# A gated cross-attention and expert layer on one core: new orders within a slot, the first two tiles' queries by one projection and transfers, and fewer identity matmuls

## The reference

```python
# x [32,128,128], ctx [32,77,96], 16 heads of 8
x = x + tanh(g_xattn) * xattn(layernorm(x), ctx)      # layer norms, q, k, v, softmax over 77 keys
x = x + tanh(g_ffn) * ffn(layernorm(x))
# ffn: logits = x @ w_router; top 2 of 8 experts, gates = softmax of the two
#      y_e = square(relu(x @ w1[e])) @ w2[e];  out = sum of gate_e * y_e
```

## Time and profile before

| | us |
|---|---|
| median of 3 runs | 349.1 (348.03 to 349.65) |
| the profiled execution, whole | 348.87 |
| its span | 347.1 |
| TensorE busy | 292.9 (84%) |
| VectorE busy | 230.6 (66%) |
| ScalarE busy | 181.0 (52%) |
| GpSimd busy | 109.2 (31%) |
| mean granted TensorE clock (1 is full) | 0.966 |

### The profile page before, as it was taken

The page is one execution under the profiler, slowest core; times in us unless marked ns, Lnnn a source line. Parts: engine busy times, 40 slices in busy tenths (PEclk is TensorE's granted clock), DMA queues, the critical chain, the costliest instruction groups (busy, mean ns, idle before and its releaser), DMA issues.

```text
span 347.1 us, 7792 instructions
## 1 busy us (share of the span) xinstructions
PE 292.9 (84%) x2809; PEld 237.6 (68%) x2809; DVE 230.6 (66%) x929; ACT 181.0 (52%) x412; POOL 109.2 (31%) x198
## 2 busy tenths in 40 slices
PE   0867979888889998999899989999999999787695
PEld 0435658666767877777777777777777788675484
DVE  7565275677757775778677757886657656554555
ACT  1331354656455566555655566466556555553373
POOL 6495305147303531343134313421322100211000
PEclk9995587999999999999999999999999999999999
DMA  3243011027343836283629281835273530350011
GB/s 82 79 128 111 19 42 34 17 54 129 118 178 57 126 111 213 53 132 105 216 49 124 54 281 35 117 66 157 115 113 54 153 126 3 81 198 0 0 34 30
DMA packets 18918, 32.92 MB, mean 95 GB/s; under 512 B 4921, under 2 KB 12058, under 8 KB 18880
## 3 DMA queue, kind: packets, MB, share of 16 engines
q1 hardware_dynamic: 12176, 23.39, 28.0%
q0 software_dynamic: 3216, 7.66, 9.2%
q10 hardware_dynamic: 3488, 1.38, 1.5%
HBM read 21.04 MB, written 2.21 MB: 67 GB/s over the span
## 4 chain that ended last, share of the span: by engine, by line
PE 46%; DVE 27%; issue 9%; DMA 6%; ACT 6%; POOL 3%; SPq 2%; DVEq 0%; ACTq 0%; POOLq 0%
PE y L592 10%; PE c L547 8%; DVE u L1122 6%; PE ab L503 4%; DMA gb<-gates_scratch 3%; PE ab L570 2%; DMA qs<-q_lo 2%; PE ab L445 2%; DVE negm L1003 2%; POOL rs L1288 2%; PE s L524 2%; PE ab L453 2%; PE ab L562 2%; PE h L478 2%; PE h L458 2%
## 5 line engine op out<-in xcount | busy, mean ns | idle before, releaser
L1003 DVE TENSOR_REDUCE negm<-ab 128x4 f32<-128x308 f32 x128 | 60.6, 474 | 53.3 <-PE ab L503 52.8
L804 ACT ACTIVATE p<-s 77x512 f32<-77x512 f32 x128 | 74.2, 583 | 17.2 <-PE s L524 17.0
L592 PE MATMUL y<-w2s,hs 128*128 128x128 f32 x448 | 61.0, 280 | 8.2 <-ACT hs L809 8.2
L524 PEld LDWEIGHTS s<-qs,ks 104*77 104x77 f32 x512 | 55.7, 153 | 13.1 <-issue 5.7
L592 PEld LDWEIGHTS y<-w2s,hs 128*128 128x128 f32 x448 | 55.3, 193 | 11.0 <-ACT hs L809 10.3
L524 PE MATMUL s<-qs,ks 104*77 104x128 f32 x512 | 59.7, 241 | 2.0 <-ACT p L804 1.8
L503 PE MATMUL ab<-ks,qs 96*128 96x312 f32 x128 | 51.4, 403 | 4.9 <-DMA qs<-q_lo 1.3
L1286 POOL TENSOR_SCALAR rs<-mv 128x1 f32<-128x1 f32 x32 | 7.4, 230 | 131.3 <-DVE mv L1044 131.2
L809 ACT ACTIVATE hs<-u 128x512 f32<-128x512 f32 x56 | 34.6, 624 | 18.0 <-DVE u L1122 17.8
L1122 DVE SCALAR_TENSOR_TENSOR u<-h,gb 128x512 f32<-128x512 f32 x56 | 36.9, 674 | 1.5 <-DMA gb<-gates_scratch 1.5
L547 PE MATMUL c<-p,vs 77*32 77x128 f32 x1024 | 34.6, 276 | 1.8 <-DVE qs L992 1.8
(11 more groups left out here) (127 smaller groups left out, 498.3 us busy)
## 6 DMA issues: line engine op xcount, KB each, us to landing
gb<-gates_scratch SPq DMA_DIRECT2D x14, 768.0 KB, 6.2
gb<-gates_scratch SPq DMA_DIRECT2D x7, 512.0 KB, 4.3
qs<-q_hi SPq DMA_DIRECT2D x12, 256.0 KB, 5.7
ks<-k_hi SPq DMA_DIRECT2D x60, 39.0 KB
x_res<-in_x_dram POOLq DMA_DIRECT2D x8, 256.0 KB, 7.4
out_dram<-y_out POOLq DMA_DIRECT2D x7, 256.0 KB, 6.4
x_sb<-in_x_dram POOLq DMA_DIRECT2D x6, 256.0 KB, 4.8
qs<-q_lo SPq DMA_DIRECT2D x6, 256.0 KB, 7.3
```

The costliest lines, as they stand in the source:

```text
L524: mm = nc.tensor.matmul(p[0:N, T * i:T * i + T], ks[:, par, c, i, NP * j:NP * j + N], qs[:, par, c, T * j:T * j + T], start=True, stop=True)
L592: mm = nc.tensor.matmul(bank_y[:, D * b:D * b + D], hs[:, e % 2, T * b:T * b + T], w2s[:, e, :], start=(e == 0 and b == 0), stop=(e == E - ...
L804: nc.scalar.activation(p32[:, m % LR, :], src, ACT.Exp).then_inc(p_done, 1)
L1003: nc.vector.tensor_reduce(negm[:, :, c], bank_ab[bank][:, 0:J * NP].rearrange("t (i n) -> t i n", n=NP)[:, :, 0:N], AX.X, ALU.max, negate= ...
```

## The change

1. **Queries of tiles 0 and 1.** `project_query_rows`, `split_query_rows`, `low_query_rows`, the weights `wq_rows` and the turned bias are gone. Both tiles now take `project_queries`, `evacuate_q`, `low_queries` and the transfers of `stack_q`, as the other tiles do. For tile 1 SP issues them, after its `stack_k`; for tile 0 ACT does, ahead of the load of the expert weights. In the bank table `q` of tile 1 stands behind `mT2`.
2. **Identity matmuls.** The 19 of steps 0 and 1 are gone; three are added behind tile 0's query projection. Those of step -1 stay.
3. **DVE order.** In slot 1 the steps of `gate` alternate with those of `attended`; in slot 2 a score maximum of `near[3]` stands between the two `gated`; in slot 3 `routed` comes before the last maximum, and `normalise2` before `q_lo` and the second `gated`. Steps 8 and 9 get their own `closing` order, with the first `gated` ahead of `attended`. DVE clears the value tile of tile 0 in place of POOL.
4. **ACT order.** In slot 1 `exponent(.., 2)` comes before `evacuate_v` and `max_store`; steps 8 and 9 square experts first.
5. **PE order.** Only from slot (7, 1) on: `values` before `turn`, `output` before `gates_turn`, `turn_heads` before `route`, the output of expert 0 held to the next slot. `turn` of batch 2 now waits at its claim.
6. **POOL order.** `load_rows` comes after `rstd` and `norm_rstd`.

```diff
-            if 0 <= step + shift < tiles and (name, step + shift) not in (("q", 0), ("q", 1))]
+            if 0 <= step + shift < tiles]
...
             def closing(j, near, ffn):                       # PE
                 if near[-1]:
-                    turn(*near[-2])
                     for c in range(NC):
                         values(*near[-1], c)
+                    turn(*near[-2])
...
-                    route(*near[-2])
                     turn_heads(*near[-1])
+                    route(*near[-2])
                 if e[2] is not None:
                     hidden(sf, pf, e[2])
+                if e[1] is not None:
+                    (output_alone if last(sf) else output)(sf, pf, e[1])
                 if near[-2] and not near[-1]:
                     route(*near[-2])
-                if e[1] is not None:
-                    (output_alone if last(sf) else output)(sf, pf, e[1])
...
+                    values_first = i == S - 1 and j > 1      # PE, step
+                    if values_first:
+                        for c in range(NC):
+                            values(*near[-1], c)
                     if near[-2]:
                         turn(*near[-2])
+                    if i == S - 1 and j == 3:
+                        output(held[0], held[1], held[2] - 1)
...
-                    if i == 0 or (i == 1 and j < 2):
-                        keep_on(bank_h[0], 2)
...
-                        (project_queries if made[0] >= 2 else project_query_rows)(made[0])
+                        project_queries(made[0])
+                    if (i, j) == (-2, 3):
+                        keep_on(bank_s2[1], 3)
...
-                    if (i == 0 and j > 0) or (i == 1 and j < 2):
-                        keep_on(bank_h[1], 2 if i else 1)
...
+            def closing(j, near, ffn, gating, post):          # DVE
+                sf, pf, held, e = ffn
+                if held and last(held[0]):
+                    weighed(*held)
+                if e[1] is not None and not last(sf):
+                    gated(sf, pf, e[1])
+                take(post, 4)
+                if near[-1]:
+                    routed(*near[-2])
+                    take(post)
+                elif near[-2]:
+                    low_x(*near[-2])
+                if e[2] is not None and not last(sf):
+                    gated(sf, pf, e[2])
+                if near[-1]:
+                    normalise2(*near[-1])
+                    low_x(*near[-2])
+                elif near[-2]:
+                    routed(*near[-2])
+                    take(gating, 7)
...
-                    if j == (2 if i == -1 else 0) and nxt:   # POOL
-                        load_rows(*nxt)
                     if near[-1]:
                         rstd(*near[-1])
                     if j == (1 if i == 0 else 0) and i != -1 and third:
                         norm_rstd(third[0], "ctx")
                         norm_rstd(third[0], "x")
+                    if j == (2 if i == -1 else 0) and nxt:
+                        load_rows(*nxt)
```

More of the change, by code:

```diff
@@ L560, in turn @@
                 pe.wait_ge(post_d, at(POST, G * s + j, "normed"))
-                p, ready = claim(s, f"turn{j}", j != 1 and not last(s))
+                p, ready = claim(s, f"turn{j}", j in (0, 3) and not last(s))
                 nc.tensor.transpose(p[:, 0:T], xn2[:, :], ident[:, :]).then_inc(ready, 1)
@@ L640, in step @@
                     sf, pf, held, e = ffn
-                    output_of = output_alone if last(sf) else output
                     if i >= S:
@@ L866, in step @@
                         load_experts()
+                    if i >= S:
+                        if near[-1]:
+                            evacuate_heads(*near[-1])
+                        for one in e[1:]:
+                            if one is not None:
+                                squared(sf, one)
+                            if one == 6 and near[-2]:
+                                evacuate_turned(*near[-2])
+                        if j == 1 and near[-2]:
+                            gate_exp(i - 1)
+                        continue
                     if near[-1]:
@@ L1214, in step @@
                     if made:
-                        prepare = chained(low_keys(*made), (low_queries if made[0] >= 2 else low_query_rows)(*made))
+                        prepare = chained(low_keys(*made), low_queries(*made))
                     if (i, j) == (-2, 3):
-                        take(prepare)
+                        take(prepare, 2)
                         take(stats(1, 1), 4)
-                        take(prepare, 9)
+                        clear_values(dve, nc.vector, 0)
+                    if i >= S:
+                        closing(j, near, ffn, gating, post)
+                        if j == 2 and not last(i - 2):
+                            finish(i - 2, par)
+                        if e[1] is not None and last(sf):
+                            weighed(sf, pf, e[1])
+                        continue
                     take(top_scores)
@@ L1244, in step @@
                     if j == 2:
+                        take(post, 2)
+                        if exists(i - 2) and i < S - 1:
+                            finish(i - 2, par)
                         take(post)
+                        if e[1] is not None:
+                            gated(sf, pf, e[1])
+                        if i == S - 1:
+                            normalise2(*near[-1])
+                        take(prepare, 2)
+                        if near[3] and i > 0:
+                            take(tops_of(near[3]))
@@ L1254, in step @@
-                    if i >= S and near[-1]:
-                        normalise2(*near[-1])
-                    if e[2] is not None and not last(sf):
-                        gated(sf, pf, e[2])
-                    take(prepare)
-                    if near[3]:
+                        if e[1] is not None and i < S - 1:
+                            gated(sf, pf, e[1])
+                        if near[-1] and i < S - 1:
+                            normalise2(*near[-1])
+                        take(prepare)
@@ L1260, in step @@
+                        if e[2] is not None:
+                            gated(sf, pf, e[2])
+                        take(prepare)
+                    if near[3] and (j != 2 or i <= 0):
                         take(tops_of(near[3]))
-                    if near[-1] and i < S:
+                    if near[-1] and (j < 2 or (j == 2 and i < S - 1) or (j == 3 and i == S - 1)):
                         normalise2(*near[-1])
```

180 lines of the change are left out of this document (75 added, 105 removed).

## The result

The changed kernel takes 345.07 us (median of 4 runs, 343.51 to 345.83), the kernel before 348.85. The ratio is 0.989, with an interval of 0.984 to 0.993. It is faster, clear of the scatter of the runs, but by 3.8 us where 15 were forecast, and outside the stated range of 328 to 341. The profiled execution took 345.51 us whole.

The account below looks back on a forecast made before the run. TensorE was taken as close to the bound, losing short waits. From 348.9 us: tiles -8.5, tail -5, first stretch -2.5, second stretch +1, giving 333.9, so 334 us; range 328 to 341 for 8 in 10.

Parts of the forecast that it names:

- Bound of the tiles, and their terms: Tiles: PE close to the bound, losing 3.0 us a tile in short waits; slots 0 to 3 save 2.0 us.
- The 1.7 that I took: Saving in us per full tile, taken below the slots' sum of 2.0; ends 0.5 and 2.4; all tiles together 8.5.
- Tail: From slot (7, 1) on: of PE's 6.8 us of waits for `hs`, 5 us go (ends 2 and 7).
- the part on slot (7, 2): Reason for taking 5 of 6.8 us in the tail: in slot (7, 2) `gb` has to land first.
- Queries of tile 0: Head: `q_lo` lands in up to 7.6 us, scores start 2.5 to 3.5 us later, first stretch ends 2.5 us sooner.
- Queries of tile 1: Step 0: row projections go, a transfer decides; 54.4 us is the limit for first scores, binding lightly or not at all.
- Identity matmuls: Steps 0 and 1: 12.0 us of PE passes go; no gain behind the `q_lo` transfer, some help in step 0.
- the clock stays down: Rival, chance 0.06: without filler PE runs at 1.2 GHz from 26 us until experts begin at about 95; 351 us.
- Second stretch: Up to the first expert gates: 0.5 us less by moving `x_res`, 1.5 lost to the clock; +1 (ends -1 and +5).
- the signs: Expected in the profile after: tile times, waits at `turn`, x transposes and `hs`, start of scores, end of `scoresT`, clock falls.
- The text's own condition for being wrong: Tile over 35 us, half clock for more than 10 us after 57, or `gb` landing last in every tile.

Follow-up runs that it names:

- rows01_filler: The changed kernel with the 19 identity matmul calls of steps 0 and 1 and the row projections for queries of tiles 0 and 1 put back; 335.4 us.

## Why the prediction was wrong

*Bound of the tiles, and their terms: right.* The waits shrink or go where they were said to. Between `turn`s of one tile the four gaps shrank by 0.39, 0.84, 0.60 and 0.47 us, against 0.4, 0.6, 0.6 and 0.4: 2.30, not 2.0. The three that were undone singly give 0.49, 0.86 and 0.59; the fourth, slot 3, was not. The 1.7 that I took was too careful. Tile 4 has no wait for `gb` in the profile of the change; where such a wait stands differs between the profiles. From `turn` of slot (2, 0) to that of (7, 1) 10.2 us went, against 7.6 by the same terms; in `rows01_filler`, where `u` waits 2.1 us for `gb` in slot (2, 2), 6.8.

*Tail: the right mechanism, too large.* Waits for `hs` after 300 us fell from 6.8 to 0.7 us, as forecast, but the tail gave 3.2 us and not 5. A new wait of 2.1 us for `p`, and a half clock behind it, took the rest; the part on slot (7, 2) named `gb`, for which `u` does wait 1.5 us there, and missed that `squared` had been moved ahead of the last exponential on ACT. With this undone the tail gives 7.1 (56.1 us before from `turn` of (7, 1), 48.97).

*Tiles and tail together* are 13.4 us against 12.6 by my terms. `rows01_filler` has them alone; its median is 13.4 us under before's, but in its profile they are 11.2, so that the median agrees to the tenth is luck.

*Queries of tile 0: the first failed step.* I took up to 7.6 us for `q_lo` "with no `x_res` beside it", from one row of tile 2. It took 9.6, and the scores began 6.05 us later, not 2.5 to 3.5. In the 7.6 us of that row 1.06 MB moved in all; in the 9.6 us here it was 1.41 MB, since the expert weights run from about 23 us on and `x_res`, issued at 23.94, stands beside it after all. The step took the time of one row for its ceiling and left out what else would travel; how much of the 9.6 us that explains is open, as said above. Both tiles' transfers together cost 5.5 us with filler where I had 2.5 us of gain; tile 0's share of it is not shown.

*Queries of tile 1: half right.* 6.8 to 7.2 us from the last issue to landing agree with the limit of 7.6. But `q_lo` was issued at 50.02 and not at 47.5. SP began its keys at 43.56 where I had 41; in the kernel before it was 42.58, so tile 0's delay is 1.0 us of it, and the rest was wrong from the start. So 54.4 became 57.5, and PE idled 6.3 us where I had it bind "lightly or not at all".

*Identity matmuls: the second failed step, and the larger.* I had them as 12 us of work with no use, and priced the clock at 1.5 us. Their removal costs 4.2 us here and 6.8 with the old queries. The rival *the clock stays down* named what happened, a half clock that lasts until the experts begin, here from about 53 us to `u` at 104.6 instead of 94.8, and got 0.06. Two things stood against it. One was 62% busy at full clock between 320 and 330 us, a stretch that had come in with full clock: that a low share can hold a full clock says nothing on what brings it back once it has fallen. The other was that step 0 at half clock "would fill PE wholly" and so get the full clock back; PE was then busy 43.5 of 47 us and did not get it. The earlier trace rows had shown that the clock falls in this head, and the trace of the kernel before has a second fall, at 50 us. The size (17 us) was too large: the whole head lost 10.0 where -2.4 was forecast, 12.4 us off, which is the whole of the error but for the 0.8 above.

*Second stretch.* Forecast +1; it came to 26.3 us from 23.4. The share of `x_res` in it can't be read off, since all of it ran at half clock.

*Of the signs*, those on waits hold: none in front of `turn` in slots 0 and 2, 0.30 in slot 1 where about 0.4 was expected, 0.33 at the transposes of x where it was 0.25, and 0.7 for `hs` after 300 us. A tile of 33.5 to 34.5 was 33.32, the first scores were to start at 23 to 24.5 and `scoresT` of tile 0 to end near 69, and came at 27.0 and 78. The text's own condition for being wrong, half clock for more than 10 us after 57, is what the trace shows.

## What to carry to other kernels

Before matmuls that do no work are taken out of a head, look for every place where the granted clock falls in it, with or without them, and ask what brings it back; a stretch that keeps a full clock with many gaps is no evidence for one that has lost it. Price a transfer by all bytes that travel beside it and the rate of rows with the same kind of transfer, count from the issue of its first piece, and take one row's time for no ceiling. Where a version differs from another by a few us, compare stretches of its profile as well as medians: here a total met its forecast with parts that did not. And when an order on one engine is changed, follow the longest wait through every engine that has something queued behind the waiter: here gates, `u`, the square and an exponential that needed none of them.

## What the runs showed of the hardware

Transfers of the queries from one on-chip buffer to another moved 118 GB/s with all 16 engines taken, weights and rows of x from memory 269 on average between 26 and 32 us. And TensorE stayed at half clock until about 103 us though busy 44 of the 47 us from 57 to 104, in two kernels (mean clock 0.50 and 0.51) that differ by 38 passes of identity matmuls from two with 0.89 and 0.93 in the same stretch. It was back at full clock at about 105 and 103 us, some 2 and 4 us behind the first matmul of the experts (102.66 and 98.31).
